# Three MLPs whose input tokens are normalised on ScalarE instead of VectorE

## What is computed

```python
def mlp(x, gain, shift, W1, b1, W2, bias):
    m, v = mean(x, -1), var(x, -1)
    n = (x - m) * rsqrt(v + 1e-5)            # the part that the change moves
    h = gelu((n * gain + shift) @ W1 + b1)   # 128 -> 512
    return h @ W2 + (x + bias)               # 512 -> 128
```

## Time and profile before

| | |
|---|---|
| median of 3 runs | 1717.77 us (1715.82 to 1717.99) |
| the profiled execution's own time | 1720.16 us |
| its span in the profile | 1718.2 us |
| mean granted TensorE clock | 0.929 of full |
| busy: PE, DVE, POOL, ACT | 1412.2, 933.5, 762.7, 690.8 us |
| MLP c, first h to last work of the phase | 540.8 to about 618 us |
| MLP e | 1065.3 to about 1149 us |
| MLP g | 1410.1 to about 1508 us |

### The profile page before, as it was taken

One profiled execution on the slowest core, in us unless ns is written; L12 is line 12 of the kernel. 1 busy time (PEld: TensorE's weight loads), 2 busy tenths in 40 slices (PEclk: granted clock), 3 DMA queues, 4 the chain that ended last, 5 costly groups with the idle time before them and its releaser, 6 DMA issues. The chain is left out here.

```text
span 1718.2 us, 46596 instructions
## 1 busy us (share of the span) xinstructions
PE 1412.2 (82%) x17965; PEld 941.0 (55%) x17966; DVE 933.5 (54%) x2357; ACT 690.8 (40%) x1421; POOL 762.7 (44%) x1343
## 2 busy tenths in 40 slices
PE   4899999999977859999999996859999978814870
PEld 2465656565545535666666664546666546603860
DVE  3465656565535955665566552965555438621431
ACT  1445454545433325555555552214443322202530
POOL 2233334343322637777777774663333224342006
PEclk9899999999997989999999997989999989956995
DMA  4430000000000310000000001210010023101115
GB/s 103 116 103 21 12 21 12 21 12 15 8 11 25 90 52 11 20 15 18 20 17 15 15 11 44 68 54 25 28 31 27 20 71 93 56 27 47 55 52 137
DMA packets 129416, 68.79 MB, mean 40 GB/s; under 512 B 20312, under 2 KB 125356, under 8 KB 129212
## 3 DMA queue, kind: packets, MB, share of 16 engines
q1 hardware_dynamic: 127164, 61.75, 12.8%
q0 software_dynamic: 2048, 4.20, 0.8%
HBM read 41.80 MB, written 24.12 MB: 38 GB/s over the span
## 5 line engine op out<-in xcount | busy, mean ns | idle before, releaser
L592 ACT ACTIVATE space<-scores 128x512 f32<-128x512 f32 x576 | 315.0, 549 | 359.2 <-PE scores L439 291.1
L678 DVE TENSOR_REDUCE space<-scores 128x2 f32<-128x512 f32 (+1 forms) x512 | 305.4, 622 | 252.6 <-PE scores L439 173.6
L410 PE MATMUL scores<-space 32*128 32x256 f32 (+1 forms) x2304 | 196.3, 410 | 26.3 <-DVE space L678 16.7
L811 POOL TENSOR_SCALAR_AFFINE_SELECT space<-space 128x512 f32<-128x512 f32 x128 | 81.4, 636 | 263.8 <-ACT space L592 263.8
L823 POOL TENSOR_TENSOR space<-space 128x1024 f32<-128x1024 f32 x64 | 151.0, 2359 | 0.0
L439 PE MATMUL scores<-space 32*128 32x256 f32 (+1 forms) x2048 | 149.2, 358 | 0.0
L410 PEld LDWEIGHTS scores<-space 32*128 32x128 f32 x2304 | 93.6, 187 | 87.0 <-DVE space L678 34.3
L815 POOL TENSOR_SCALAR_AFFINE_SELECT space<-space 128x512 f32<-128x512 f32 x128 | 81.6, 638 | 85.3 <-ACT space L592 85.3
L1444 ACT ACTIVATE space<-scores,w_later_cols 128x512 f32<-128x512 f32 x96 | 65.6, 687 | 128.5 <-PE scores L1393 126.7
L439 PEld LDWEIGHTS scores<-space 32*128 32x128 f32 x2048 | 83.3, 188 | 17.8 <-issue 0.2
L1474 DVE TENSOR_SCALAR space<-space 128x128 f32<-128x128 f32 x96 | 77.2, 864 | 18.9 <-POOL space L1590 18.9
(11 more groups left out here) (322 smaller groups left out, 3027.0 us busy)
## 6 DMA issues: line engine op xcount, KB each, us to landing
space<-in_x SPq DMA_DIRECT2D x32, 128.0 KB, 2.2
x<-space SPq DMA_DIRECT2D x16, 256.0 KB, 3.2
space<-xx SPq DMA_DIRECT2D x32, 128.0 KB, 2.2
xo<-space SPq DMA_DIRECT2D x32, 128.0 KB
space<-xo SPq DMA_DIRECT2D x16, 256.0 KB
space<-xm SPq DMA_DIRECT2D x32, 128.0 KB, 2.1
space<-x SPq DMA_DIRECT2D x16, 256.0 KB, 3.3
sorted_in<-zeros SPq DMA_DIRECT2D x10, 256.0 KB
```

The lines of the kernel that those rows point to most:

```text
L410: last = pe.matmul(a.score_bank(j)[:, 0:n], q[rows, e * P:(e + 1) * P], keys[rows, 0:n], start=not cut, stop=True, skip_group_check=True)
L592: act.activation(pt[:, 2 * pair:2 * pair + 2, lo:S], a.score_banks(pair)[:, :, S + lo:2 * S], ACT.Exp, bias=0.0, scale=1.0)\
L678: last = dve.tensor_reduce(out[:, c % 2, 2 * pair:2 * pair + 2], banks[:, :, 0:n], AX.X, ALU.max, negate=True)
L811: pool.affine_select(out=block, in_=block, compare_op=ALU.is_ge, fill=0.0, base=0, pattern=[[0, 4], [1, P]], channel_multiplier=-1).then_i ...
```

## The change

ScalarE gets a function `norm(t+2)`, called in its `body` ahead of the Gelus of step t: four activations with the function Identity, each with a per-partition scale (1/sqrt(var+eps)) and a per-partition bias (the offset). The offset is -mean/sqrt(var+eps), which GpSimd makes in two more small instructions behind its power: mean times -1 (`minus`), and that times the reciprocal root (`offset`). VectorE's `norm(t+2)` is taken out of its `body`. It stays ahead of the phases, for steps 0 and 1, and GpSimd makes their offsets too, though nobody reads them. Two semaphores and two small buffers are added.

```diff
--- before.py
+++ after.py
@@ -1266,7 +1266,7 @@
     def __init__(self, k, name, src, also, after, dst, keep, start, w):
         self.k, self.name, self.src, self.also, self.after = k, name, src, also, after
         self.dst, self.keep, self.start, self.w = dst, keep, start, w
-        each = dict(x_in=16, stored=16, stats=1, aggr=1, eps_in=1, rstd=1, wn=1, t_full=1, xt=1, h_full=FC, gelu=FC,
+        each = dict(x_in=16, stored=16, stats=1, aggr=1, eps_in=1, rstd=1, minus=1, offset=1, wn=1, t_full=1, xt=1, h_full=FC, gelu=FC,
                     y_full=1, biased=1, r=1, out=1)
         if after == "norm":
             each.update(rstats=1, raggr=1, reps=1, rrstd=1, rn=1, gained=1)
@@ -1439,6 +1439,8 @@
 
         if (due := s["y_full"].due(t, lambda x: x - 1)) is not None:
             act.wait_ge(s["y_full"].sem, due)
+        if t.reg is not None or t.n + 2 < MSTEPS:
+            norm(t + 2)
         for f in range(FC):
             act.wait_ge(s["h_full"].sem, s["h_full"].at(t, lambda x: FC * x + f + 1))
             act.activation(k.mh[:, t.parity, f], k.scores[f // 2][:, (f % 2) * 512:(f % 2 + 1) * 512], ACT.Gelu,
@@ -1446,6 +1448,16 @@
 
         if m.after == "route" and (t.reg is not None or t.n > 0):
             keep_rows(t + -1)
+
+    def norm(t):
+
+        act.wait_ge(s["offset"].sem, s["offset"].at(t, lambda x: x + 1))
+        if (due := s["t_full"].due(t, lambda x: x - 1)) is not None:
+            act.wait_ge(s["t_full"].sem, due)
+        for blk in range(MB):
+            last = act.activation(k.mwn[:, t.parity, blk], k.mx[:, t.parity, blk], ACT.Identity, bias=k.moffset[:, t.parity, blk:blk + 1],
+                                  scale=k.mrstd[:, t.parity, blk:blk + 1])
+        last.then_inc(s["wn"].sem, 1)
 
     def keep_rows(t):
 
@@ -1547,8 +1559,6 @@
             norm_stats(t + 2)
         if t.reg is not None or t.n > 0:
             normed(t + -1)
-        if t.reg is not None or t.n + 2 < MSTEPS:
-            norm(t + 2)
         if m.after == "route" and (t.reg is not None or t.n > 1):
             route_logits(t + -2)
         finish(t)
@@ -1595,8 +1605,14 @@
 def mlp_rstd(pool, m):
     k, power = m.k, mlp_power(pool, m)
 
+    s = m.s
+
     def rstd(t):
         power(k.maggr, k.meps, k.mrstd, ("aggr", "eps_in", "rstd", "wn"), t)
+        pool.tensor_scalar(k.mminus[:, t.parity], k.maggr[:, t.parity, :, 0], -1.0, None, ALU.mult).then_inc(s["minus"].sem, 1)
+        pool.wait_ge(s["rstd"].sem, s["rstd"].at(t, lambda x: x + 1))
+        pool.wait_ge(s["minus"].sem, s["minus"].at(t, lambda x: x + 1))
+        pool.tensor_tensor(k.moffset[:, t.parity], k.mminus[:, t.parity], k.mrstd[:, t.parity], ALU.mult).then_inc(s["offset"].sem, 1)
 
     return rstd
 
@@ -2043,6 +2059,7 @@
         self.ctx_in, self.cn = t(2, 64)[0:TC], t(2, 64)[0:TC]
         self.mx, self.mwn = t(2, 4, 128), t(2, 4, 128)
         self.mstats, self.maggr, self.meps, self.mrstd = t(2, 4, 6), t(2, 4, 2), t(2, 4), t(2, 4)
+        self.mminus, self.moffset = t(2, 4), t(2, 4)
         assert self.at <= SPACE, self.at
 
         self.at = 0
```

## The result

The changed kernel takes **1841.1 us** (median of four, 1839.9 to 1844.8) against 1717.9 us, a ratio of 1.0721 with a 95% interval of 1.0702 to 1.0741. That is 123 us slower. The forecast was 1834, 116 us slower, in a range of 1803 to 1860. The profiled execution after has a span of 1839.7 us and a mean granted clock of 0.906 (before 1718.2 and 0.929).

The account below looks back on a forecast made before the run. DVE was taken to bound the middle of an MLP before, ACT's wait to decide after. MLPs c +47.7, e +42.6, g +34.2 and step 6 -8.3 us sum to +116, so 1834 us, range 1803 to 1860.

Parts of the forecast that it names:

- What decides instead: where ACT has to wait.: Steps 0 to 5 of each MLP: Gelus queue behind a norm waiting for its offset, so PE idles, 18 times.
- The step of c, 14.6 us at full clock: MLP c, one h to the next through transposes, offset, four activations, Gelus and y: 14.6 us with PE at full clock.
- The estimate from the skill's figures: ScalarE's four activations by the skill's per-operand and per-element costs: 1.64 us, making the sum 2.5 us larger.
- The clock, 1.6 us a step: PE falls to 1.2 GHz in nearly every new gap, costing 0.85 to 2.6 us a step, taken as 1.6.
- Step 0 and the late table load: First step of each MLP, table load now in the chain (+1.3 us): 19.8, 20.5 and 20.5 us to the next h.
- Step 6: No norm there, so it loses its stall by DVE: 7.45, 7.5 and about 9.0 us, together -8.3.
- At nothing I cost: DVE's shorter body, extra instructions ahead of a phase, POOL's other work, SP's loads and `keep_rows`: no cost.
- The sum: Three MLPs +47.7, +42.6 and +34.2 us, step 6 -8.3: +116 us, 1834 us against the median.
- The rule against it: Skill's rule of VectorE for multiply and add; alone it would give a loss of about 4 us, near 1721.
- The rival with the wait covered, 1676 us: Offset in time, ACT loses nothing, steps fall to PE's own length: 42 us faster, 1676 us, chance 0.03.
- The range's low end: 1803 us, set to take in the rival of PE staying at 2.4 GHz through the gaps: 1805, chance 0.12.

Follow-up runs that it names:

- wait_alone: Changed kernel, but VectorE normalises in its body as before and ScalarE only waits for the offset of step t+2 ahead of the Gelus: 1811.4 us.
- offset_alone: Kernel before, plus GpSimd's two small instructions minus and offset, whose result nobody reads: 1709.7 us.
- norm_behind: Changed kernel, but ScalarE normalises step t+2 behind the Gelus of step t, not ahead of them: 1691.3 us.
- norm_next: Changed kernel, but ScalarE normalises step t+1, not t+2, ahead of the Gelus of step t: 1689.6 us.
- fill_gap: Changed kernel, plus six unread matmuls in PE's gap ahead of y, in steps 0 to 5 of MLPs c and e: 1835.8 us.
- norm_twice: Changed kernel, with ScalarE's four normalising activations of a step made twice, first into an unread spare buffer: 1872.1 us.
- the two fillings: fill_gap and fill_over, the changed kernel with unread matmuls in PE's gap: 1835.8 and 1829.4 us.
- the fast forms: The four runs norm_behind, norm_next, bias_first and next_bias_first: 1691.3, 1689.6, 1687.1 and 1687.6 us.
- norm_alone_on_port: Kernel before, plus one wait: GpSimd holds its bias of step t+1 until VectorE has made the norm of step t+2: 1705.1 us.
- bias_first: norm_behind, with GpSimd's bias of step t+1 put ahead of its power of step t+2: 1687.1 us.
- fill_over: fill_gap with nine unread matmuls instead of six and none in step 0: 1829.4 us.
- next_bias_first: norm_next, with GpSimd's bias of step t+1 put ahead of its power of step t+2: 1687.6 us.

## Why the prediction was right

- **"What decides instead: where ACT has to wait."** Right, and shown from both sides: with the wait alone the time is 91 us above the kernel before and 102 us above the same kernel without it (wait_alone, offset_alone), and the work without the long wait costs nothing and gains 28 to 31 us (norm_behind, norm_next). The order of events was as written, line by line.
- **The step of c, 14.6 us at full clock.** Measured with the clock kept up: 14.97 (fill_gap). The four activations take 1.65 us, not 1.50. From the end of the power (565.77) to the start of the first activation (566.36) are 0.59 us where I had 0.51. The rest is behind the last Gelu, in y.
- **The estimate from the skill's figures.** An estimate from the Trainium skill ("ScalarE: Activation LUTs", What ACT_TABLE_LOAD costs) had given 1.64 us for the four, against my 1.50 by width between two PSUM rows. The trace agrees with it: 478 ns at the median for one and 1.65 us for four. My 1.50 left out that the four read SBUF; whether that is why it was low was not tested. By that estimate the sum would have been 1836.5.
- **The clock, 1.6 us a step.** The mechanism was right: 0.79 to 0.80 in every window of steps 1 to 5. The size was a little low: about 1.9 in c and e. The reason given, "PE falls to 1.2 GHz in nearly every one of the new gaps", holds but is not all of it: with the gap filled but for 1.0 to 1.8 us the clock still fell in 6 of 10 steps behind step 0. With y paced by the Gelus, short holes can be enough, though they are not always: the four steps that kept the clock had holes of 1.15 to 1.37 us, inside the same span, so the length of the hole does not tell which step falls.
- **Step 0 and the late table load.** 19.8, 20.5 and 20.5 forecast, 18.9, 19.5 and 19.8 measured: about 0.9 us too long each. The table load did come behind the first norm, and cost its 1.3 us. Most of the error is luck: the h of step 0 was itself shorter than before (in c the transposes started 5.07 us after it, not 5.75), 2.2 us over the three MLPs. The change does not touch that h, and in c it lasted 5.23 us here and 5.87 to 6.70 in the traces of wait_alone, norm_twice and the two fillings.
- **Step 6.** 7.45, 7.5 and 9.0 forecast, 7.45, 7.45 and 8.78 measured.
- **"At nothing I cost"** GpSimd's other work, SyncE's loads and `keep_rows`: nothing of it is on the chain of the step. In this kernel; in the fast forms the loads and GpSimd are what remains.
- **The sum.** +116 forecast, +123 measured (+121 in the spans). Of the spans' 5 us, steps 1 to 5 were 0.6 us too short in c and e and 0.3 in g (7.6 in all: ACT's 0.15, the hand-overs, the clock's 0.3), step 0 was 2.7 too long over the three. So the sum came out closer than its terms, by errors of opposite signs. The other 2 us are between span and median.
- **The rule against it** (the Trainium skill, "ScalarE: Activation LUTs", Rules for kernel authors: VectorE for multiply and add). The skill's figure there is for bf16, and this kernel is float32. The trace speaks against using it here: contended, VectorE took 4.10 us for what ScalarE does in 1.65, and with the wait out of the way ScalarE's version is 28 to 31 us faster. Uncontended (norm_alone_on_port) VectorE needs 1.12 us and the rule holds for the instructions themselves; even so that kernel, at 1705.1, is some 15 us slower than norm_next.
- **The rival with the wait covered, 1676 us.** It is what the two orders of norm_behind and norm_next make real. Its size was 14 us too good: I had VectorE as the only thing ahead of PE, and in e the loads and GpSimd come next.
- **The range's low end,** with PE at 2.4 GHz, was not needed: the profile has no step at full clock between 0 and 5 (0.72 to 0.80 in all three MLPs).

## What to carry to other kernels

Before work goes to a less busy engine, follow its operands back to the engine that waits for what is queued behind it: if the chain comes round within one step, the loop turns serial, and the price is the length of that chain and not of the work. Here one wait without any work cost 102 us against the same kernel without it, and the same instructions, off that chain, gained 30. Look also at which instructions of a slow engine run beside GpSimd's long ones, since keeping them apart gained 13 to 15 us without moving any work. How much of the 30 us is the end of that overlap, and how much the shorter list of VectorE, was not separated.

## What the runs showed of the hardware that was not expected

- VectorE's `tensor_scalar` from SBUF to SBUF on 128 x 128 floats took 336 to 348 ns with GpSimd kept off it, and up to 1426 ns beside GpSimd's 128 x 512 additions and multiplications. Two more small GpSimd instructions, which delay the long ones by some 0.5 us, made the kernel some 10 us faster; the median of a block fell from 1278 to 346 ns with them.
- The granted clock fell to 1.2 GHz in 6 of 10 steps of fill_gap in which PE had been idle for only 1.0 to 1.8 us and then worked in four short pieces, each behind a Gelu. In the other 4, idle for 1.15 to 1.37 us, it did not fall. With no hole, it stayed at 2.4 GHz. In the changed kernel the fall comes inside the gap, and the clock is back some 5 us after PE's restart:

```profile
581.80:582.80 1.00, 0.00 (x0) 0.00 (x0) 0.00 (x0) 0.03 (x1) 0.85 (x4) 1.00 0.00 0
...
583.80:584.80 1.00, 0.00 (x0) 0.00 (x0) 0.00 (x0) 1.00 (x3) 1.00 (x2) 0.50 0.00 0
...
588.80:589.80 1.00, 1.00 (x7) 1.00 (x6) 0.00 (x0) 0.00 (x0) 0.00 (x0) 0.50 0.02 6
...
590.80:591.80 1.00, 1.00 (x9) 0.92 (x9) 0.07 (x1) 0.00 (x0) 0.00 (x0) 1.00 0.00 0
```

- In the profiled execution of bias_first the clock came back late at the start of the cross attention. In windows of 1 us PE is busy all through from 1136 us on (with small matmuls, many of 32 x 64 or 128 x 256); the clock is 0.50 until 1148, 1.00 for some 4 us, and 0.50 again from 1153 to about 1172.5. So it fell once, and stayed low for 19 us, with no idle time of PE to be seen in the windows before. It is not a matter of the fast forms alone: fill_over shows the same at 1228 to 1250, with some 4 us at 1.00 in the middle. The time of next_bias_first varied by 21 us between executions. None of this is explained.
